# Cross-attention block with 16 experts: the gathered rows are turned by VectorE and transfers inside SBUF instead of TensorE

## What is computed

```python
x = x + xattn(layernorm(x), ctx, ctx, Wq, Wk, Wv, Wo)
h = layernorm(x)
scores = softmax(h @ gate_w.T).transpose(0, 2, 1)
topk_w, topk_idx = top_k(scores, 64)
x_tok = take_along_axis(h, topk_idx)              # 16 experts, 8 x 64 = 512 rows each
eo = (gelu(x_tok @ Wg.T) * (x_tok @ Wu.T)) @ Wd.T * topk_w
x = x + scatter_add(eo) + shared(h)
```

## Time and profile before

| | us |
|---|---|
| median of three runs | 1428.64 (1427.55 to 1428.79) |
| the profiled execution, its own time | 1423.46 |
| its span, first to last instruction | 1421.7 |
| PE busy | 1360.4 (96%) |
| ACT busy | 957.4 (67%) |
| DVE busy | 647.7 (46%) |
| POOL busy | 211.2 (15%) |
| mean granted TensorE clock | 0.988 of full speed |

### The profile page before, as it was taken

The page is one execution under the profiler, slowest core; times in us unless marked ns, Lnnn a source line. Parts: engine busy times, 40 slices in busy tenths (PEclk is TensorE's granted clock), DMA queues, the critical chain, the costliest instruction groups (busy, mean ns, idle before and its releaser), DMA issues.

```text
span 1421.7 us, 22246 instructions
## 1 busy us (share of the span) xinstructions
PE 1360.4 (96%) x8906; PEld 783.3 (55%) x8906; DVE 647.7 (46%) x1294; ACT 957.4 (67%) x1073; POOL 211.2 (15%) x173
## 2 busy tenths in 40 slices
PE   4879999999999999999999999998999999999995
PEld 3434444444444435344444443325888888888885
DVE  4434244234235324424523531204449677777772
ACT  3547988888888887888888889994232344444441
POOL 1000000000000000000000000020000336666654
PEclk9989999999999999999999999999999999999998
DMA  6473765586387478467548627623343465666653
GB/s 171 122 164 112 118 126 148 107 150 156 101 136 161 127 124 147 137 118 149 146 109 135 170 69 122 134 73 133 132 132 108 134 175 148 150 151 148 149 97 38
DMA packets 97160, 185.82 MB, mean 131 GB/s; under 512 B 16992, under 2 KB 51296, under 8 KB 97056
## 3 DMA queue, kind: packets, MB, share of 16 engines
q1 hardware_dynamic: 80768, 154.08, 45.5%
q0 software_dynamic: 16000, 29.91, 10.2%
q10 hardware_dynamic: 288, 0.39, 0.2%
HBM read 118.99 MB, written 61.83 MB: 127 GB/s over the span
## 4 chain that ended last, share of the span: by engine, by line
PE 86%; ACT 4%; DVE 4%; issue 2%; DMA 2%; SPq 1%; POOL 0%; POOLq 0%; DVEq 0%
PE acc L1291 24%; PE score L1331 18%; PE score L1267 17%; PE score L1346 9%; PE misc L1182 6%; PE misc L1195 5%; ACT probs L679 4%; PE misc L1218 2%; PE misc L1203 2%; PE misc L1210 1%; DMA key_scr<-key_parts 1%; PE misc L1226 1%; DVE o_sum L859 1%; SPq L388 1%; PE acc L1358 1%
## 5 line engine op out<-in xcount | busy, mean ns | idle before, releaser
L679 ACT ACTIVATE probs<-score 128x1024 f32<-128x1024 f32 (+1 forms) x832 | 789.4, 1043 | 162.8 <-PE score L1267 158.0
L1291 PE MATMUL acc<-probs,values 128*32 128x512 f32 (+1 forms) x3328 | 411.2, 600 | 4.5 <-DVE o_sum L859 3.3
L1267 PE MATMUL score<-queries,keys 48*128 48x512 f32 (+1 forms) x1664 | 315.2, 451 | 3.4 <-DMA keys<-key_parts 2.4
L1267 PEld LDWEIGHTS score<-queries,keys 48*128 48x128 f32 (+1 forms) x1664 | 128.3, 180 | 258.1 <-ACT probs L679 201.5
L688 ACT ACTIVATE gelu<-score 128x512 f32<-128x512 f32 x96 | 57.1, 594 | 209.9 <-PE score L1331 209.8
L1291 PEld LDWEIGHTS acc<-probs,values 128*32 128x32 f32 (+1 forms) x3328 | 82.9, 109 | 183.8 <-issue 143.6
L576 POOL DMA_DIRECT2D ctx_raw<-ctx_t x32 | 23.4, 731 | 754.7 <-DVE ctx_lo L767 753.8
L778 DVE CAST key_parts<-misc 128x512 fp32r<-128x512 f32 (+1 forms) x63 | 36.2, 574 | 206.9 <-PE misc L1182 195.4
L1331 PE MATMUL score<-tok_hi,gu_hi 128*128 128x512 f32 x384 | 119.8, 393 | 0.0
L1331 PE MATMUL score<-tok_lo,gu_hi 128*128 128x512 f32 x384 | 119.3, 392 | 0.0
L1331 PE MATMUL score<-tok_hi,gu_lo 128*128 128x512 f32 x384 | 118.7, 391 | 0.0
(11 more groups left out here) (158 smaller groups left out, 1382.5 us busy)
## 6 DMA issues: line engine op xcount, KB each, us to landing
keys<-key_scr SPq DMA_DIRECT2D x180, 200.2 KB, 8.0
key_scr<-key_parts SPq DMA_DIRECT2D x45, 512.0 KB, 4.4
gu_raw<-w_gu SPq DMA_DIRECT2D x17, 1024.0 KB, 6.4
ctx_raw<-ctx_t POOLq DMA_DIRECT2D x24, 512.0 KB, 4.1
queries<-query_scr SPq DMA_DIRECT2D x180, 64.0 KB, 2.7
d_raw<-w_d SPq DMA_DIRECT2D x17, 512.0 KB, 9.0
query_scr<-query_parts SPq DMA_DIRECT2D x15, 512.0 KB, 4.5
xn<-x SPq DMA_DIRECT2D x8, 512.0 KB, 3.8
```

Source lines behind the costliest of these rows:

```text
L679: act.activation(probs[0:rows, n % RING, 2 * pair:2 * pair + 2, :], score[k % 3][0:rows, :, :], ACT.Sigmoid, scale=SCALE).then_inc(probs_d ...
L1267: mm = pe.matmul(score[k % 3][0:rows, g, :], keys[quarter % KEY_RING][of, pair, P * st:P * st + rows], queries[half][of, e, pair, :], star ...
L1291: mm = pe.matmul(acc[32 * c:32 * (c + 1), :], values[b % 2][0:rows, st, half, c, :], probs[0:rows, n % RING, c, :], start=(st == 0), stop= ...
```

## The change

From expert 2 on TensorE no longer turns the gathered rows. `turn(e)` on VectorE transposes the gathered tile in blocks of 32 x 32 (one instruction over 128 x 1024 elements) into `blocks`, which is the tile xn. `place(e)` on SyncE then moves the 4 x 4 combinations of 32-row blocks to their partitions with 16 transfers from SBUF to SBUF (xn to norm, 32 partitions x 2 x 128 elements each, 32 KB). `turned_tokens(e)` on VectorE reads them from norm and splits them into tok_hi and tok_lo. Experts 0 and 1 (DIRECT_ROWS = 2) keep TensorE's transposes. Gathers run five experts ahead instead of three, and the scaling of the finished rows moves from VectorE (line 1026) to ScalarE (`expert_result`).

```diff
+            def place(e):
+                sp.wait_ge(turned, e + 1 - DIRECT_ROWS)
+                wait_past(sp, tok_split, e - DIRECT_ROWS)
+                for i in range(BLOCKS):
+                    for j in range(BLOCKS):
+                        sp.dma_start(tok_raw[TURN * j:TURN * (j + 1), :, P * i:P * (i + 1)],
+                                     blocks[TURN * i:TURN * (i + 1), j::BLOCKS, :]).then_inc(placed, 16)
...
             for n in range(1, B + 1):
+                if n == B:
+                    sp.wait_ge(set_split, 4)
+                    load_weights(3, 1)
+                    place(2)
...
-            for s in range(3, SETS):
-                sp.wait_ge(set_split, 2 * s - 2)
-                load_weights(s, s % 2)
+            for e in range(1, E):
+                if e + 3 < SETS:
+                    sp.wait_ge(set_split, 2 * e + 4)
+                    load_weights(e + 3, (e + 1) % 2)
+                if e + 2 < E:
+                    place(e + 2)
...
-                if before:
+                if e >= 2 + DIRECT_ROWS:
+                    pool.wait_ge(turned, e - 1 - DIRECT_ROWS)
+                elif e >= 2:
                     pool.wait_ge(tok_full, TABLES + KC * (e - 1))
...
+            def expert_result(e, par):
+                act.wait_ge(adds_ready, 2 * e + 1)
+                for t in range(TT):
+                    act.wait_ge(d_full, 2 * (e + B) + t // 2 + 1)
+                    last = act.activation(result[par][:, t, :], d_bank[:, t // 2, D * (t % 2):D * (t % 2 + 1)],
+                                          ACT.Copy, scale=add_w[par][:, t:t + 1])
+                    if t % 2:
+                        last.then_inc(scaled, 1)
...
+            def turn(e):
+                par = e % 2
+                dve.wait_ge(rows_in[par], 8 * TT * (e - par) + 16 * TT)
+                wait_past(dve, placed, PLACE_DMAS * (e - DIRECT_ROWS))
+                dve.transpose(blocks.rearrange("p j (t q) -> p t j q", q=TURN),
+                              gathered[par][:].rearrange("p t (j q) -> p t j q", q=TURN)).then_inc(turned, 1)
+
+            def turned_tokens(e):
+                par = e % 2
+                dve.wait_ge(placed, PLACE_DMAS * (e + 1 - DIRECT_ROWS))
+                for k in range(KC):
+                    raw = tok_raw[:, k, :].rearrange("p (i t q) -> p t i q", i=BLOCKS, q=TURN)
+                    hi = tok_hi[par][:, k, :].rearrange("p (t i q) -> p t i q", i=BLOCKS, q=TURN)
+                    lo = tok_lo[par][:, k, :].rearrange("p (t i q) -> p t i q", i=BLOCKS, q=TURN)
+                    dve.tensor_copy(hi, raw).then_inc(tok_step, ts.up())
+                    dve.wait_ge(tok_step, ts.now())
+                    last = dve.tensor_tensor(lo, raw, hi.bitcast(F32), ALU.subtract)
+                last.then_inc(tok_split, 1)
...
             def expert(e, par):
                 hidden_quarters(n, par, (0, 1))
-                if more_tokens:
+                if e + 1 < DIRECT_ROWS:
                     tokens(1 - par)
+                    rows_of(e + 3, 1 - par, True)
+                elif e + 1 < E:
+                    turned_tokens(e + 1)
+                if e + 2 < E:
+                    turn(e + 2)
+                if e + 4 < E:
+                    rows_of(e + 4, par, True)
```

More of the change, by code:

```diff
@@ L40 @@
 STACK_DMAS = 16 * 2 * len(KEY_PART)
+TURN = 32
+BLOCKS = P // TURN
+PLACE_DMAS = 16 * BLOCKS ** 2
+DIRECT_ROWS = 2
 E, F, CAP = 16, 512, 64
@@ L271, in build @@
             logits = sb("logits", [P, TT, B, E])
+        blocks = xn[:].rearrange("p t d -> p (t d)").rearrange("p (j c) -> p j c", c=P)
+        tok_raw = norm[:].rearrange("p t d -> p (t d)").rearrange("p (k s) -> p k s", s=S)
         last_out = logits[0:E].rearrange("p t b e -> p (t b e)")
@@ L334, in build @@
         d_copied = sem("d_copied")
+        scaled = sem("scaled")
         tok_full = sem("tok_full")
         tok_copied = sem("tok_copied")
+        turned = sem("turned")
+        placed = sem("placed")
         tok_step = sem("tok_step")
+        tok_split = sem("tok_split")
         soft_step = sem("soft_step")
@@ L612, in _, with gather @@
             split_lo(1, 0, 0)
-            def gather(e, par, before):
+            def gather(e, par):
                 pool.wait_ge(post_stored, STORE * B)
                 pool.wait_ge(rows_ready, e + 1)
-                if before:
+                if e >= 2 + DIRECT_ROWS:
+                    pool.wait_ge(turned, e - 1 - DIRECT_ROWS)
+                elif e >= 2:
                     pool.wait_ge(tok_full, TABLES + KC * (e - 1))
@@ L637, in add_rows @@
                     ).then_inc(added[par], 16)
-            gather(0, 0, False)
-            gather(1, 1, False)
-            gather(2, 0, True)
+            for e in range(5):
+                gather(e, e % 2)
             for e in range(E):
-                if e + 3 < E:
-                    gather(e + 3, (e + 1) % 2, True)
+                if e + 5 < E:
+                    gather(e + 5, (e + 1) % 2)
                 add_rows(e, e % 2)
@@ L1022, in expert_result @@
                                 ).then_inc(adds_ready, 1)
[L1023 to L1030, removed]
             def rows_of(e, par, before):
@@ L1163, in expert @@
                 else:
-                    expert_result(e - 1, 1 - par)
+                    expert_rows(e - 1, 1 - par)
                 hidden_quarters(n, par, (2, 3))
-                if more_tokens:
+                if e + 1 < E:
                     set_lo(1, par, e + 2)
             for e in range(E):
-                expert(e, e % 2, e + 1 < E, e + 2 < E)
-            expert_result(E - 1, 1)
+                expert(e, e % 2)
+            expert_rows(E - 1, 1)
         @block.tensor
@@ L1394, in _, with expert @@
                         product(AFTER[2 + k])
-            def expert(e, par, more):
+            def expert(e, par):
                 n, slot = e + B, 1 - par
                 pe.wait_ge(set_split, 2 * e + 3)
-                pe.wait_ge(tok_copied, TABLES + KC * e + KC)
+                if e < DIRECT_ROWS:
+                    pe.wait_ge(tok_copied, TABLES + KC * e + KC)
+                else:
+                    pe.wait_ge(tok_split, e + 1 - DIRECT_ROWS)
                 up(n, par, slot, (0, 1))
-                if more:
+                if e + 1 < DIRECT_ROWS:
                     transpose_rows(e + 1, 1 - par)
@@ L1407, in _ @@
             for e in range(E):
-                tf.n = TABLES + KC * e + KC
-                expert(e, e % 2, e + 1 < E)
+                expert(e, e % 2)
             pe.wait_ge(set_split, 2 * SETS)
```

19 lines of the change are left out of this document (12 added, 7 removed).

## The result

Over four runs the changed kernel takes 1414.34 us (1409.64 to 1417.39), the kernel before 1428.22 us (1427.55 to 1428.79). The ratio is 0.990, with a 95% interval of 0.987 to 0.9931: 1% faster, 13.9 us between the medians. The forecast was 1416 with a range of 1414.5 to 1434.

A forecast was written before the change was run, and what follows sets the result against it. The prediction took PE, busy 96% of the span, as the bound. Removing 12.5 us of transposes and 0.5 us of waiting from the 1428.64 us median gave 1415.6, forecast as 1416 us, range 1414.5 to 1434.

The forecast's parts named there:

- PE's bound and what goes: TensorE in the experts: busy 96%, sets the time; fourteen transpose steps (12.5 us) and 0.5 us of gather wait go.
- VectorE: VectorE's load per expert: tokens 2.12 us, transpose 1.2, scaling gone; 12.1 us of a 16.66 us period, so it fits.
- The bounds of 0.6 and 2.28 for the transpose: VectorE's transpose of the gathered tile, taken as 1.2 us: lower end 0.6, upper end 2.28 us.
- ScalarE: ScalarE's four scalings ahead of the gelu of quarter 2: 0.42 us each, 1.7 in all, with nothing on PE waiting.
- the other estimate: ScalarE's scaling priced from the Trainium skill's ACTIVATE costs: 0.40 us each, leaving the conclusion as it is.
- 1.1 us to spare: ScalarE's gelu of quarter 2: done at 15.6 us into the expert, its bank needed by PE at 16.66.
- The loop through SyncE: Turn, sixteen issues, landing, token split: 16.3 us, to fit PE's 16.66 us period with 0.4 us spare.
- Rival 3: SyncE's transfers land one behind another: loop 40.2 us, +316 us, 1745 us; chance 0.02.
- The rest is free: SyncE's later weight loads and store_unit(7), GpSimd's gathers and the program's end: moved or waiting, at no cost in time.
- The sum: Whole kernel: 13.0 us less, 1410.4 us from the profiled execution, 1415.6 on the median, rounded to 1416.
- the low end: Bottom of the range for the whole kernel's time: 1414.5 us, if nothing is lost, with the spread of the runs.
- The term for the spread: Allowance for run-to-run spread of the whole kernel's time, within the 1414.5 us end of the range; put at about 1.1 us.

The follow-up runs named there:

- scale_dve: The changed kernel with the scaling of finished rows back on VectorE; 1414.34 us, ratio 0.9908 to the kernel before.
- two_queues: The changed kernel with the scaling back on VectorE and four of the sixteen transfers issued by ScalarE; 1415.03 us, ratio 0.9911 to the kernel before.
- no_turn: The kernel before with the scaling on ScalarE and gather row numbers put down one expert earlier, TensorE still turning all rows; 1426.25 us, ratio 0.9994.
- turn_twice: The changed kernel with VectorE's 32 x 32 transpose done twice in a row per expert; 1427.31 us, ratio 0.9997 to the kernel before.
- no_place: The changed kernel without the 16 transfers per expert and the waits for them, so with wrong numbers; 1415.26 us, ratio 0.9905 to the kernel before.
- again: The changed kernel run once more with no edit; 1410.56 us, ratio 0.989 to the kernel before.
- split16: The changed kernel with all 16 transfers per expert cut in two, 32 issues for the same bytes; 1538.67 us in one run.
- split4: The changed kernel with four of the 16 transfers per expert cut in two, 20 issues for the same bytes; 1437.33 us in one run.

## Why the prediction was right, and where its range failed

- **PE's bound and what goes.** Right. The forecast took 13.0 us off PE; scale_dve and two_queues reach 13.05 and 13.08 in the stretch, the kernel after 12.33. The split into 12.5 of transposes and 0.5 of waiting agrees with no_turn: 0.85 us for the earlier gather with the slow first half of that step, 12.3 for the rest.
- **VectorE.** Transpose 1.24 us (forecast 1.2), the four token instructions 1236.39 - 1234.26 = 2.13 (2.12), load 12.20 (12.1). The bounds of 0.6 and 2.28 for the transpose were not needed; turn_twice shows what the upper one would have meant.
- **ScalarE.** Four scalings take 1.57 us (forecast 1.7), 0.39 each in a row, against 0.42 taken and 0.40 in the other estimate. The "1.1 us to spare" was right in kind: the gap takes up what comes late, and only the latest expert, in which DVE waited 1.27 us for the parts, passes it by much, with 0.63 us on PE. That it costs anything needs both a late transfer (no_place: no loss in the turned experts) and the scaling ahead of the gelu (scale_dve: no loss).
- **The loop through SyncE.** Issue 0.68 us each in the expert shown (10.81/16, forecast 0.63), landing 3.1 (forecast 2.8), so place is 1251.57 - 1237.63 = 13.9 us there; in the next expert, from the end of the transpose at 1255.22 to the tok_hi at 1268.22, it is 13.0, as forecast. (The 0.1 us for the semaphore, a term for which the prediction shows no row, is 0.03 here, from 1237.63 to 1237.66.) From tok_hi to tok_hi that is 17.3 us (1234.26 to 1251.57) and 16.65; the mean of 13 is 16.72. Rival 3 is out: sixteen transfers in flight take 10.81 + 3.1 us and not sixteen landings. The loop was put at 16.3 with 0.4 to spare; it lies about at PE's period of 16.66, now above and now below, and DVE waits for a transfer 8 times, which the forecast said it would not. The time came out right since the excess does not pile up: a late expert is followed by one that catches up, and PE needs the tokens only an expert later. How near the edge this is, four more issues show: from 0.7 us lost to 25.7 more.
- **The rest is free.** Right for SP and for store_unit. POOL's gathers got longer, 1.30 us each against 0.98 over the whole span, and do so without the transfers too (no_place: 1.26); this used up some of its slack and reached nobody.
- **The sum.** On the median the forecast was 13.0 us less, and 13.9 came. The mechanism was right and the central value 1.7 us from the median. That the medians agree so well is partly luck: the changed stretch brought 12.3 us, and the runs of again show 16.4 between the medians.
- **The step that failed** is the low end, "1414.5 (nothing lost, and the spread of the runs)". It is the 1415.6 of the sum less 1.1 us, about the 1.24 by which the three runs before differed. The working itself had the number that speaks against this: the profiled execution, 1423.46 us, lay 5.2 us under the median and 4.1 under the lowest of the three, so three runs did not show the spread. The term for the spread, put at about 1.1 us, is mis-sized: the start of the program alone varies by 6.9 us (1099.7 to 1106.6) and the clock of the last down by 1.5 us (7.50 or 5.99), and runs of one kernel spread over 7 to 8 us in four of the sets above (after, again, and the kernel before in its 25 and 11 runs), though its 7 runs on the third chip stayed within 1.5. A median of four from such a spread moves by 2 us or so, as the two medians of the same kernel show (1414.34 and 1410.56). With that the low end would have been, as an estimate from these runs, 1411 or lower.

What stays open: why the granted clock of the first stages and of the last product differs between executions of the same code. The runs show that it does and what it costs, and not what decides it. That the late start comes from the clock is read from the windows of single executions and was not tested by an edit; in again, which starts latest of all, the clock is 1.00 from 20 to 30 us and 0.52 from 30 to 40.

## What to carry to other kernels

Work that is taken off the bounding engine and sent through another engine and a DMA queue forms a loop; its length (here turn, sixteen issues, one landing, split) has to fit into the bounding engine's period, and the load of each engine alone does not tell whether it does. The price of many small transfers was here the number of issues times some 0.65 us on one queue, and issuing on two queues shortened such a loop; it pays only where the loop is longer than the period, for with one transpose it changed nothing. Before giving a range for a time, look at how far the profiled execution lies from the other runs of the same kernel, and measure the changed stretch between two marks of its own, since the part that was not touched may move by more than the change is worth.

## What the runs showed of the hardware

- A transfer of 32 partitions x 2 x 512 bytes inside SBUF takes 0.64 to 0.68 us of issue on SP, one of half the bytes 0.65 (split16); ScalarE issues the same at 0.71 us in parallel with SP.
- The landing of the last of them differs from run to run and expert to expert: 3.1 and 2.8 us in the kernel after, 1.4 in split4, 1.2 in split16. What it meets there was not taken apart.
- Sixteen transfers of 32 KB per expert raise the DMA engines' busy share over 14 periods from 0.61 (no_place) to 0.74 (after), and the rate from 144 to 176 GB/s. GpSimd's gathers are 1.26 and 1.30 us there, and 0.98 in the kernel before.
- VectorE's transpose of 32 x 32 blocks over 128 x 1024 float32 elements takes 1.24 us, as long as a pass of the same size that subtracts (1.23).
- Behind the same 2.21 us of idle TensorE the last 48 products took 7.50 us in some executions and 5.99 in others. In the kernel before, their first 3.3 us ran at a granted clock of 0.53; in the kernel after, all of them ran at 1.00.
